# Routing ranks and softmax rewritten, one bias step, the block table and the first expert blocks reordered, in a gated cross-attention and mixture-of-experts kernel

## The reference

```python
# layer 0: 8 small experts (256 -> 128 -> 256), 2 of 4 groups, then 4 experts of 8, and a shared one
group_scores = sum(top_k(grp, 2)[0]); grp_idx = top_k(group_scores, 2)[1]
topk_idx = top_k(where(score_mask, scores_c, 0.0), 4)[1]
# layer 1: 8 large experts (256 -> 1024 -> 256), the best 2 of 8 for every row
logits = x @ Wr + br
_, top_idx = top_k(logits, 2)
mask = any(top_idx[..., None] == arange(8), axis=-2)
weights = softmax(where(mask, logits, -1e9))
out = sum over e of (relu(x @ W1[e] + b1[e]) @ W2[e] + b2[e]) * weights[:, :, e]
x = x + tanh(g_ffn[1]) * out
```

## Time and profile before

| | |
|---|---|
| median of 3 runs | 1090.82 us (1088.45 to 1092.29) |
| profiled execution, its own time | 1095.5 us |
| its span on the core | 1093.4 us |
| PE / DVE / ACT / POOL busy | 86% / 70% / 44% / 20% |
| granted TensorE clock, mean | 0.891 of full speed |

### The profile page before, as it was taken

One profiled execution on the slowest core, in us unless ns is written; L12 is line 12 of the kernel. 1 busy time (PEld: TensorE's weight loads), 2 busy tenths in 40 slices (PEclk: granted clock), 3 DMA queues, 4 the chain that ended last, 5 costly groups with the idle time before them and its releaser, 6 DMA issues.

```text
span 1093.4 us, 17999 instructions
## 1 busy us (share of the span) xinstructions
PE 940.4 (86%) x6385; PEld 746.0 (68%) x6385; DVE 767.0 (70%) x1609; ACT 479.8 (44%) x834; POOL 219.9 (20%) x388
## 2 busy tenths in 40 slices
PE   3468999999999998899988777885469999999995
PEld 2345677777767666666655454543369999999995
DVE  2544576776676667788777679873658888888882
ACT  1124544444443432333333334432147667666762
POOL 2011210110110000001000013201124455445423
PEclk9766799999999999999999866765569999999998
DMA  4996663254253235456262973240365667767752
GB/s 115 211 223 143 103 122 71 59 85 80 49 88 67 49 80 89 105 108 146 60 145 80 188 162 89 71 142 24 109 230 177 211 209 237 231 195 232 236 151 29
DMA packets 121336, 142.16 MB, mean 130 GB/s; under 512 B 11456, under 2 KB 105560, under 8 KB 121120
## 3 DMA queue, kind: packets, MB, share of 16 engines
q1 hardware_dynamic: 112416, 128.77, 47.0%
q0 software_dynamic: 8832, 12.25, 5.2%
HBM read 109.97 MB, written 31.01 MB: 129 GB/s over the span
## 4 chain that ended last, share of the span: by engine, by line
PE 59%; DVE 20%; issue 7%; ACT 4%; DMA 4%; SPq 2%; POOL 1%; DVEq 0%; POOLq 0%; ACTq 0%
PE bank L930 12%; PE bank L769 7%; PE by_query L914 7%; PE by_key L914 6%; DVE rowmax L1241 4%; DVE clipped L1266 4%; PE bank L779 4%; PE value_bank L713 3%; PE bank L624 3%; PE bank L740 3%; PE by_query L677 3%; PE by_key L698 2%; PE bank L663 2%; PE bank L633 2%; DMA lower<-max 2%
## 5 line engine op out<-in xcount | busy, mean ns | idle before, releaser
L1241 DVE TENSOR_REDUCE rowmax<-by_query 128x4 f32<-128x1024 f32 x128 | 155.7, 1216 | 22.9 <-PE by_query L677 22.8
L1055 ACT ACTIVATE probs<-clipped 128x1024 f32<-128x1024 f32 x64 | 67.6, 1057 | 182.8 <-DVE clipped L1266 182.8
L1696 POOL TENSOR_SCALAR rstd<-moments 128x2 f32<-128x2 f32 x32 | 7.1, 223 | 580.7 <-DVE moments L1205 580.7
L1747 POOL DMA_INDIRECT out_x<-x,token_i x46 | 77.4, 1682 | 157.2 <-ACT x L1160 147.2
L930 PE MATMUL bank<-w_hi,h_hi 128*128 128x256 f32 x368 | 104.1, 283 | 0.0
L930 PE MATMUL bank<-w_lo,h_hi 128*128 128x256 f32 x368 | 104.1, 283 | 0.0
L930 PE MATMUL bank<-w_hi,h_lo 128*128 128x256 f32 x368 | 104.1, 283 | 0.0
L677 PE MATMUL by_query<-stack_k,stack_q 48*128 48x256 f32 x512 | 70.7, 357 | 30.0 <-DVE rowmax L1241 24.9
L1266 DVE SCALAR_TENSOR_TENSOR clipped<-by_key,lower 128x512 f32<-128x512 f32 x128 | 82.0, 682 | 12.7 <-DMA lower<-max 11.2
L677 PEld LDWEIGHTS by_query<-stack_k,stack_q 48*128 48x128 f32 x512 | 43.0, 207 | 69.8 <-issue 35.7
L698 PE MATMUL by_key<-stack_q,stack_k 50*128 50x256 f32 x512 | 67.6, 346 | 25.0 <-DVE clipped L1266 20.4
(11 more groups left out here) (237 smaller groups left out, 2227.1 us busy)
## 6 DMA issues: line engine op xcount, KB each, us to landing
w<-in_L_ffn_W SPq DMA_DIRECT2D x46, 1024.0 KB, 8.8
lower<-max SPq DMA_DIRECT2D x64, 256.0 KB, 3.5
stack_k<-qk SPq DMA_DIRECT2D x96, 128.0 KB, 4.8
stack_q<-qk SPq DMA_DIRECT2D x96, 128.0 KB, 7.2
qk<-hi SPq DMA_DIRECT2D x32, 256.0 KB, 3.4
qk<-lo SPq DMA_DIRECT2D x32, 256.0 KB, 4.3
rows<-w_gate SPq DMA_DIRECT2D x8, 264.0 KB, 3.7
x<-in_x SPq DMA_DIRECT2D x8, 256.0 KB, 5.3
```

Of the source, the lines that this page charges most:

```text
L1055: ac.activation(probs[i % 4][:, :, :, :].rearrange("p h k s -> p (h k s)"), src, ACT.Exp).then_inc(sem.exp_done, 1)
L1241: dv.tensor_reduce(rowmax[u % 2][:, 2 * p:2 * p + 2, :], by_query[:, :, :].rearrange("p h (t s) -> p h t s", t=TT), AX, ALU.max).then_inc( ...
L1747: po.indirect_dma_start(out[:, :], bass.IndirectOffsetOnAxis(ap=token_i[:, n:n + 1].bitcast(U32), axis=0), ysb[i % 3][:, t, :], None, comp ...
```

## The change

1. `rank_of` is cut in two. `compare` makes the two 0/1 tables and multiplies the first by `before`, waiting only for the first table; `count_before` takes the larger of the two (no product with `after`) and sums. The constant `after` is gone from SBUF and from POOL's start.
2. `logits1` takes the maximum over all eight logits and subtracts it before the ranks are counted, so ACT's exponential runs beside the counting; the three operations that put -1e9 outside the mask are gone. `weights1` multiplies the exponentials by the mask, sums, inverts, and does the two scalings in one operation.
3. The first part of `tables` becomes a stage `blocks`, planned one half step earlier and ahead of the last `weights1`.
4. `bias_turn` and `bias1` of sequence 7 of 8 move five half steps later (319 to 324, 321 to 326).
5. On ACT and DVE `split_w1(1)` comes ahead of `split_rows(0)`, on ACT `split_w1(0)` comes ahead of the bias copy; `up(0)` and `hidden(0)` are run in two halves, with `turn_rows(1)` and `split_rows(1)` between them.

```diff
+        if b == NB - 1:
+            at[g + 11].append(("blocks", 0))
+            at[g + 12].append(("tables", 0))
         at[g + 11].append(("weights1", b))
-        if b == NB - 1:
-            at[g + 12].append(("tables", 0))
-        at[g + 13].append(("bias_turn", b))
-        at[g + 15].append(("bias1", b))
+        late = 5 if b == NB - 2 else 0
+        at[g + 13 + late].append(("bias_turn", b))
+        at[g + 15 + late].append(("bias1", b))
...
         turn_rows(0)
-        up(0)
+        up(0, range(0, 2))
         turn_rows(1)
+        up(0, range(2, 4))
...
-        ac.wait_ge(sem.b1_mm, 1)
-        ac.activation(b1_all[:, :, :].rearrange("p j b -> p (j b)"), down_bank[1][:, 0:JH * BLOCKS], ACT.Copy).then_inc(
-            sem.b1_ready, 1)
...
         split_w1(0)
+        ac.wait_ge(sem.b1_mm, 1)
+        ac.activation(b1_all[:, :, :].rearrange("p j b -> p (j b)"), down_bank[1][:, 0:JH * BLOCKS], ACT.Copy).then_inc(
+            sem.b1_ready, 1)
+        split_w1(1)
         split_rows(0)
-        hidden(0)
+        hidden(0, range(0, 2))
         split_rows(1)
+        hidden(0, range(2, 4))
         split_w2(0)
-        split_w1(1)
...
+        def compare(values_ap, n):
...
             linked()
             link(dv.tensor_tensor(pa, j, i, ALU.is_ge))
+            first_half = links[0]
             link(dv.tensor_tensor(pb, j, i, ALU.is_gt))
+            dv.wait_ge(sem.route_chain, first_half)
+            link(dv.tensor_tensor(pa, pa, bef, ALU.mult))
+
+        def count_before(ranks, n):
...
             linked()
-            link(dv.tensor_tensor(pa, pa, bef, ALU.mult))
-            link(dv.tensor_tensor(pb, pb, aft, ALU.mult))
-            linked()
-            link(dv.tensor_tensor(pa, pa, pb, ALU.add))
+            link(dv.tensor_tensor(pa, pa, pb, ALU.max))
             linked()
             link(dv.tensor_reduce(ranks, pa, AX, ALU.add))
             linked()
...
-            rank_of(lg, r1[:, 1, :, :], E1)
+            compare(lg, E1)
+            link(dv.tensor_reduce(r1[:, 7, :, 0], lg, AX, ALU.max))
+            linked()
+            dv.tensor_tensor(r1[:, 2, :, :], lg, r1[:, 7, :, 0:1].broadcast_to([P, TT, E1]),
+                             ALU.subtract).then_inc(sem.soft_ready, 1)
+            count_before(r1[:, 1, :, :], E1)
...
             dv.wait_ge(sem.exp1_done, b + 1)
-            link(dv.tensor_reduce(r1[:, 7, :, 1], r1[:, 3, :, :], AX, ALU.add))
+            dv.wait_ge(sem.mask_ready, b + 1)
+            link(dv.tensor_tensor(r1[:, 4, :, :], r1[:, 3, :, :], mask[:, tiles, :], ALU.mult))
+            linked()
+            link(dv.tensor_reduce(r1[:, 7, :, 1], r1[:, 4, :, :], AX, ALU.add))
             linked()
             link(dv.reciprocal(r1[:, 7, :, 2], r1[:, 7, :, 1]))
             linked()
-            link(dv.tensor_scalar(r1[:, 7, :, 3], r1[:, 7, :, 2], tg[:, 3:4], None, ALU.mult))
-            linked()
-            link(dv.tensor_tensor(r1[:, 4, :, :], r1[:, 3, :, :], r1[:, 7, :, 3:4].broadcast_to([P, TT, E1]), ALU.mult))
-            linked()
-            dv.tensor_tensor(wide_rows[b % 4][:, :, D:WIDE], r1[:, 4, :, :], mask[:, tiles, :], ALU.mult).then_inc(
+            dv.scalar_tensor_tensor(wide_rows[b % 4][:, :, D:WIDE], r1[:, 4, :, :], tg[:, 3:4],
+                                    r1[:, 7, :, 2:3].broadcast_to([P, TT, E1]), ALU.mult, ALU.mult).then_inc(
                 sem.weights1_done, 1)
```

More of the change, by code:

```diff
@@ L187, in share_banks @@
             if stage in ("load", "stack", "stats", "normal", "take", "groups0", "ranks0", "weights0", "any_nan",
-                         "reload", "load_alternative", "pick_z", "soft1", "count1", "weights1", "tables") or (stage == "ctx" and layer_of(n)):
+                         "reload", "load_alternative", "pick_z", "soft1", "count1", "weights1", "blocks", "tables") or (stage == "ctx" and layer_of(n)):
                 continue
@@ L232, in build @@
     before = sb("before", [P, 8, 8])
-    after = sb("after", [P, 8, 8])
     keep_row = sb("keep_row", [P, 1], I32)
@@ L899, in turn_rows, with up @@
             tr.then_inc(sem.xs_turned, 1)
-        def up(i):
+        def up(i, which=range(JH // 2)):
             (h1, l1), (xh, xl) = w1_split[i % 2], xs_split[i % 3]
@@ L904, in up @@
             pe.wait_ge(sem.w1_lo, i + 1)
-            for pair in range(JH // 2):
+            for pair in which:
                 if i:
@@ L1138, in split_rows, with hidden @@
                           ACT.Copy).then_inc(sem.xs_hi, 1)
-        def hidden(i):
+        def hidden(i, which=range(JH // 2)):
             if i == 0:
@@ L1303, in project @@
                                         ALU.add).then_inc(sem.z_ready, 1)
-        def rank_of(values_ap, ranks, n):
+        def compare(values_ap, n):
             j = values_ap.unsqueeze(2).broadcast_to([P, TT, n, n])
@@ L1313, in rank_of @@
             link(dv.tensor_tensor(pa, j, i, ALU.is_ge))
+            first_half = links[0]
             link(dv.tensor_tensor(pb, j, i, ALU.is_gt))
+            dv.wait_ge(sem.route_chain, first_half)
+            link(dv.tensor_tensor(pa, pa, bef, ALU.mult))
+        def count_before(ranks, n):
+            pa, pb = (pairs[:, side, :, 0:n, 0:n] for side in range(2))
             linked()
-            link(dv.tensor_tensor(pa, pa, bef, ALU.mult))
-            link(dv.tensor_tensor(pb, pb, aft, ALU.mult))
-            linked()
-            link(dv.tensor_tensor(pa, pa, pb, ALU.add))
+            link(dv.tensor_tensor(pa, pa, pb, ALU.max))
             linked()
@@ L1322, in rank_of @@
             linked()
+        def rank_of(values_ap, ranks, n):
+            compare(values_ap, n)
+            count_before(ranks, n)
         def row(i):
@@ L1485, in tabled, with blocks @@
             dv.wait_ge(sem.table_chain, chain[0])
-        def tables(_):
+        def blocks(_):
             dv.wait_ge(sem.counted, NB)
@@ L1511, in tables @@
             dv.tensor_scalar(onehotT[:, :], block_e[:, :], part_no[:, 0:1], None, ALU.is_equal).then_inc(sem.onehotT_ready, 1)
+        def tables(_):
             table(dv.tensor_tensor(slots_all[:, :, :], by_query[:, 0, 0:NT * E1].rearrange("p (t e) -> p t e", e=E1),
@@ L1556, in _ @@
                   "weights0": weights0, "gate_up": gate_up, "down0": down0, "any_nan": any_nan, "spread_nan": spread_nan,
-                  "mean_project": mean_project, "pick_z": pick_z, "logits1": logits1, "weights1": weights1, "tables": tables}
+                  "mean_project": mean_project, "pick_z": pick_z, "logits1": logits1, "weights1": weights1, "blocks": blocks, "tables": tables}
         for g in range(SLOTS_IN_ALL):
@@ L1666, in _ @@
         triangle(before[:, :, :], 8, [[1, 8], [-1, 8]], 0)
-        triangle(after[:, :, :], 8, [[-1, 8], [1, 8]], 0)
         triangle(tri[:, :], P, [[1, P]], -1)
```

10 lines of the change are left out of this document (removed).

## The result

| | before | changed |
|---|---|---|
| median of the runs compared | 1092.16 us (1088.45 to 1092.88, 6 runs) | 1076.88 us (1072.56 to 1083.70, 6 runs) |
| ratio, 95% interval | | 0.987 [0.9847, 0.9893] |
| profiled execution / its span | 1095.5 / 1093.4 us | 1083.7 / 1081.9 us |
| granted TensorE clock, mean | 0.891 | 0.890 |
| DVE busy, instructions | 767.0 us, 1609 | 757.0 us, 1553 |

The forecast was 1075.6, from 1069.5 to 1082.5. The median went down by 15.3 us, against 15.2 forecast. The profiled execution is the slowest of the six and went down by 11.8 only.

A forecast was written before the change was run, and what follows sets the result against it. It took waits, not PE's work, to bound the time where attention ends and expert blocks start. Terms 9.5 + 1.7 + 1.0 + 3.0 = 15.2 us off the 1090.82 median gave 1075.6 us, range 1069.5 to 1082.5.

The forecast's parts named there:

- First blocks: Start of the expert blocks: splitting w1(1) earlier removes PE's waiting and low clock before down(0); 9.5 us off.
- so up(0) still starts at 795.15, and costs nothing more: First expert block: the earlier w1 splits fit idle time, so up(0) is not delayed; otherwise 2.3 us later.
- Late next: First expert blocks: DVE becomes the late engine, and PE loses 0.3 us waiting for w1_lo(2).
- the three loads delay w2(0): First blocks' lower bound: w2(0) comes last of three loads under way, giving 8.0 us instead of 9.5; not taken.
- Bias of sequence 7 of 8: Last sequence's finish: moving the bias step lets pick_z start at 756.05 instead of 757.78; 1.7 us off.
- Last routing and tables: From last logits to slots on DVE: shorter routing and an earlier block table start slots at 774.31; 1.0 us off.
- the smaller sum: Routing priced with semaphore waits costing nothing extra, by the Trainium skill: total gain half a microsecond smaller.
- Routing of the other sequences: Layers 0 and 1, middle sequences: shorter routing gives 1.3 + 1.7 = 3.0 us off, bounds 0 and 5.1.
- (a): Middle of the kernel: PE swallows the savings there; 12.2 us off, 1078.6; chance 0.2.
- (b): Expert start: late weights or DVE make PE wait 2 to 5 us; gain 10 to 13, 1078 to 1081; chance 0.12.
- (c): First expert blocks: the gap isn't the weights' doing and comes back whole; gain 5.7, 1085; chance 0.04.
- (e): Whole kernel: all chain steps count, more than the sum; 17.3 us off, 1073.5; chance 0.12.

The follow-up runs named there:

- e5: The changed kernel run a second time, unaltered, for its spread and a second trace; 1076.63 us, ratio 0.9864.
- e1: The kernel before with only the new order of the first expert blocks; 1086.63 us, ratio 0.9956.
- e9: The changed kernel without the shorter ranks and the new layer 1 softmax and weights; 1083.58 us, ratio 0.9904.
- e4: The kernel before with shorter ranks, softmax beside them, shorter weights, and the block table ahead of the last weights; 1082.42 us, ratio 0.9917.
- e8: The kernel before with the shorter ranks alone, layer 1 softmax and weights as before; 1087.45 us, ratio 0.9947.
- e12: The kernel before with shorter ranks, softmax and weights in layer 1 only, layer 0 ranking as before; 1085.56 us, ratio 0.9931.
- e3: The kernel before with only shorter ranks, softmax beside them and shorter weights; 1083.26 us, ratio 0.9913.
- e7: Like e3 against the kernel before, but the unused constant `after` is still allocated and built; 1081.92 us, ratio 0.991.
- e6: The changed kernel, but DVE splits w1(0) only after block 0's rows have landed, and w1(1) after splitting those rows; 1077.37 us, ratio 0.9848.
- e10: e6 with SP also waiting for the rows of block 1 ahead of the second-layer weights; 1073.49 us, ratio 0.9813.
- e11: e10 with DVE waiting only until POOL has issued both gathers of block 0, not for the rows; 1074.32 us, ratio 0.9845.

## Why the prediction was right, point by point

**First blocks: the mechanism right, the term too large.** Up(0) to down(0) fell to 15.26 in the changed kernel (forecast near 15), with 15.38, 15.54 and 14.97 in e5, e1 and e9, mean 15.3. In the seven traces without edit 5 it is 23.4 to 24.71, mean 23.8, and the 24.71 is the trace of before: up(1) took the 8.67 us of the earlier trace rows there, against 7.8 in e4. So the price was read from one execution at its worst, 0.9 too much. The rest is the step "so up(0) still starts at 795.15, and costs nothing more": rows to up(0) is 9.52 to 9.61 in four traces with edit 5 and 8.21 to 8.22 in seven without. The working had asked whether w1(0) lands in time and whether DVE comes free; it did not ask what POOL does during DVE's split, which it put at 787.2 to 789.5, though the first gather's issue stands at 788.10 in the trace of before. Row numbers to down(0) went from 32.0 on average (7 traces) to 24.85 (4 traces), 7.1 us instead of 9.8; row numbers to the end of the span from 305.5 to 298.7, **6.8 us instead of 9.5**.

**Late next: DVE, as named.** PE waited 0.59 us for w1_lo(2) in the changed kernel (forecast 0.3), with DVE at 11.67 of 12.00, and hardly at all in e5. That the three loads delay w2(0) did not happen: in e5 it lands at 783.72, 5.9 us after its issue, while the third load lands at 793.03. The working's "all three have landed by about 806.3" was wrong by 1.7 us (the third lands at 807.96 in the trace of before), but w2(0) was not the one that came last.

**Bias of sequence 7 of 8: right in kind, 1.1 instead of 1.7.** Pick_z followed z by 0.13 us. The moved addition (line 1442) ran at 757.60, for 0.66 us, while POOL worked on the statistics from 757.84 on: the cover named was there.

**Last routing and tables: 1.07 instead of 1.0.** The size is right (6.85 to 5.78), the parts are not: edits 1 and 2 alone give 1.35, and edit 3, which the working counted among the gains, takes 0.29 back. The wait of a dependent step was priced right: 0.32 between 766.86 and 767.18, and between 767.18 and 767.50, against the 0.20 and 0.21 of independent steps, so the smaller sum, which gave such a wait no price, is out by these rows. The "larger of" took 0.28, as the addition it replaced.

**Routing of the other sequences: too small, about 6 instead of 3.0.** The step that failed is the one that took DVE's time on the chain of one trace as the upper bound, 5.1 us, and then a part of it. Layer 0 in units 2 to 8 came out as priced: the chain of before (its places as in the earlier trace rows) passes two routings there, 2 x 0.52 = 1.04 at most, and 0.9 came. In units 8 to 12 it passes three, 1.6 at most, and 2.5 came. In layer 1 the bound was 3 x 0.85 = 2.5, and 4.0 came: seven routings run between unit 13 and z, not three, and DVE's busy time there fell from 100.1 to 100.3 us to 94.5 to 94.8, by some 5.5 (e8, ranks alone: 98.2). That savings off the chain counted as well fits this, but is not shown: e8 saved only 2.0 on DVE there and took 128.9, no longer than the others.

Part of the excess in units 8 to 12 goes with the clock. The stretch from unit 8 to 9, in before, e12, the changed kernel and e5, in this order:

```profile
381.45:434.11 52.66, 46.16 (x265) 33.53 (x265) 37.44 (x94) 16.76 (x34) 4.23 (x16) 0.94 0.42 87
381.67:433.22 51.55, 47.63 (x265) 34.30 (x265) 37.35 (x95) 16.68 (x34) 4.23 (x16) 0.90 0.46 89
380.50:432.74 52.24, 46.40 (x265) 33.40 (x265) 36.92 (x93) 16.78 (x34) 4.24 (x16) 0.93 0.44 88
377.10:427.45 50.35, 44.83 (x265) 32.19 (x265) 36.88 (x92) 16.67 (x34) 4.26 (x16) 0.97 0.48 91
```

At a granted clock of 0.93 to 0.94 it takes 52.6 to 52.7 with the long ranks (three traces) and 52.1 to 52.3 with the short ones (four), so DVE's steps are worth 0.4 to 0.5 there. The other two long ones (e9, e12) have 0.90 and 51.5: their clock falls once, earlier, and for longer, and is back ahead of the eight products shown under e5. The other five short ones have 0.97 and 50.1 to 50.6. So the clock is at 0.97 in 5 of 9 traces with short ranks and in none of 5 without. That a shorter DVE step ends PE's pauses sooner and so keeps the clock up more often fits this, but is argued, from few traces; no run set the pause alone. From unit 13 to z the clock says nothing: its mean is 0.64 to 0.68 with the edits and 0.62 to 0.67 without, and 125.1 us came at 0.65, 132.3 at 0.67. Why the end of attention varies by 6.5 us between executions of one kernel (131.6 and 125.1) stays open.

**The sum.** 6.8 + 1.1 + 1.07 + about 6 = 15.0, against 15.3 by the medians, 14.2 by the ratio (its interval 11.7 to 16.7) and 15.2 forecast. Two terms were too large by 3.3 together and one too small by about 3, so that the total came within 0.1 us is luck; the 6 is also the least known of the four and in part taken from the totals.

**The rivals.** (a), PE swallowing the middle, is out, as e3, e7 and e8 are faster by 5.8 to 9.8. (b), PE waiting 2 to 5 us for a late feed: PE waits 0.71 and 0.59 in the changed kernel and 0.97 and 0.06 in e5, so it is out as a size. The larger wait has a cause that it did not name, rows asked for late; what it named, DVE behind, is the 0.59. (c) is out: PE's gap ahead of up(1) is 6.92 to 7.84 us in all seven traces without edit 5, and no gap in the first blocks is over 0.97 in the seven with it. (d), slower, is out: from the second half of up(0) 24 products take 2.88. (e) was the closest in the routing alone. The mark "if up(0) starts less than 3 us earlier, the routing part is wrong" was badly set: it started 2.5 us earlier in the changed kernel's first trace and 15.4 earlier in its second (779.71), with the same kernel.

## What to carry to other kernels

- Price a gap from several executions where there are any, and as a distance between two marks; a place in the span carries all the noise of what lies before it.
- When a large DVE operation is moved, look at what GpSimd issues at that time, not only at inputs and free engines; moving it again (e6) only chose which gathers it held.
- Where PE and DVE wait for each other in turn, the chain of one trace is no upper bound for what a shorter DVE step gives: count the step wherever it runs (seven times here, three of them on the chain as priced). Two edits that fill the same wait don't add up (1.35 with one, 1.07 with both).

## What the runs showed of the hardware that was not expected

- A subtraction of 128x2048 fp32 on DVE (2.3 us) stretches an indirect gather's issue on POOL from 0.94 to 1.24 us to 1.89 to 2.78, in each of the 21 cases in 14 traces where the issue starts inside it; an issue that starts first, or with it, keeps 0.94 to 0.98.
- Small row gathers beside megabyte loads on another queue can land late: from the end of the issue 1.81 us for the second gather in the changed kernel, 5.77 (e5), 5.79 (e10) and 6.13 (e11) for the gather that the chain goes through there. In e10 and e11 the loads under way are the two second-layer matrices and the first-layer one of block 2; which of them does it was not separated.
- The granted clock after the same kind of pause is not the same from one execution to the next: the same eight products take 2.77 and 1.97 us in the changed kernel's two traces. Its times run from 1070.19 to 1083.70 us in twelve runs; how much of that is the clock was not separated.
